# RWKV-6 time mixing and a ternary feed-forward on one core: a diagonal block copied earlier on GpSimd, and two elementwise steps moved from VectorE to GpSimd

## What is computed

```python
xx = x_prev - x                                  # difference of neighbouring tokens
mix = tanh((x + xx * time_maa_x) @ maa_w1)       # then, by five small matmuls, mw, mk, mv, mr, mg
xw, xk, xv, xr, xg = (x + xx * (time_maa_i + m_i) for each i)
r, k, v, g = xr @ Wr.T, xk @ Wk.T, xv @ Wv.T, silu(xg @ Wg.T)
decay = exp(-exp(time_decay + tanh(xw @ td_w1) @ td_w2))
# per token and head: y = r (S + u k v'),  S = decay * S + k v'
y = group_norm(y) * ln_g + ln_b
x = layernorm(x + (y * g) @ Wo.T)
h = layernorm(gelu(x @ ternary(W_fc).T)) @ ternary(W_proj).T
out = layernorm(x + h)
```

## Time and profile before

| | |
|---|---|
| median of 3 runs | 3076.63 us (3074.3 to 3081.04) |
| the profiled execution: own time | 3077.73 us |
| the profiled execution: span | 3075.9 us |
| PE busy | 2895.1 us (94%) |
| DVE busy | 2488.6 us (81%) |
| ACT busy | 1928.0 us (63%) |
| POOL busy | 931.3 us (30%) |
| granted TensorE clock, mean over the span | 0.991 |

### The profile page before, as it was taken

One profiled execution on the slowest core, in us unless ns is written; L12 is line 12 of the kernel. 1 busy time (PEld: TensorE's weight loads), 2 busy tenths in 40 slices (PEclk: granted clock), 3 DMA queues, 4 the chain that ended last, 5 costly groups with the idle time before them and its releaser, 6 DMA issues.

```text
span 3075.9 us, 101635 instructions
## 1 busy us (share of the span) xinstructions
PE 2895.1 (94%) x40249; PEld 2120.9 (69%) x40249; DVE 2488.6 (81%) x5435; ACT 1928.0 (63%) x4079; POOL 931.3 (30%) x790
## 2 busy tenths in 40 slices
PE   1889999999999999999999999999999999999997
PEld 0666677777677777677777676777677777767775
DVE  8467887788887788888788898788798788888777
ACT  0456676666676666676666576666567666667664
POOL 1223232333322333332233322233323233332232
PEclk9899999999999999999999999999999999999999
DMA  5000000000000000000000000000000000000000
GB/s 215 8 15 23 13 19 23 22 16 22 13 23 19 23 16 23 16 20 19 23 16 22 16 19 19 23 15 22 23 13 19 23 22 16 23 13 23 19 23 15
DMA packets 22822, 73.40 MB, mean 24 GB/s; under 512 B 3104, under 2 KB 3360, under 8 KB 20768
## 3 DMA queue, kind: packets, MB, share of 16 engines
q1 hardware_dynamic: 22432, 67.10, 6.4%
HBM read 50.31 MB, written 16.78 MB: 22 GB/s over the span
## 4 chain that ended last, share of the span: by engine, by line
PE 63%; DVE 23%; issue 9%; ACT 3%; DVEq 1%; DMA 1%; SPq 0%; ACTq 0%; POOLq 0%; POOL 0%
PE psP L404 18%; PE psF L641 11%; PE psP L442 7%; PE psP L616 6%; PE psF L660 4%; DVE HLO L1351 4%; DVE ARENA L1226 2%; PE psY L522 2%; PE psY L538 2%; DVE SUMS L1343 2%; DVE ARENA L1100 2%; DVE ARENA L1088 2%; DVE ARENA L1166 2%; DVE ARENA L1290 1%; PE psP L424 1%
## 5 line engine op out<-in xcount | busy, mean ns | idle before, releaser
L404 PE MATMUL psP<-ARENA,WALL 128*128 128x256 f32 x3072 | 694.2, 381 | 2.7 <-ACT ARENA L733 2.7
L690 ACT ACTIVATE ARENA<-ARENA 32x512 f32<-32x512 f32 (+3 forms) x930 | 524.2, 564 | 188.1 <-DVE ARENA L1166 92.5
L404 PEld LDWEIGHTS psP<-ARENA,WALL 128*128 128x128 f32 x3072 | 574.9, 190 | 79.3 <-issue 1.8
L1351 DVE SCALAR_TENSOR_TENSOR HLO<-GG,FWB,HHI 128x128 f16<-128x128 f32 x1024 | 347.5, 400 | 283.4 <-ACT HHI L861 278.4
L641 PE MATMUL psF<-XHI,WFC 128*128 128x128 f16 x4096 | 488.2, 220 | 2.2 <-DVE ST L1367 1.9
L641 PE MATMUL psF<-XLO,WFC 128*128 128x128 f16 x4096 | 486.6, 220 | 0.0
L902 POOL TENSOR_TENSOR MT<-ARENA 32x256 fp32r<-32x256 f32 x330 | 319.3, 968 | 445.3 <-ACT ARENA L690 416.7
L916 POOL TENSOR_TENSOR ARENA<-ARENA,XT 128x1024 f32<-128x1024 f32 x128 | 278.6, 2177 | 506.3 <-DVE ARENA L1100 506.3
L641 PEld LDWEIGHTS psF<-XHI,WFC 128*128 128x128 f16 x4096 | 397.9, 98 | 41.0 <-issue 32.9
L641 PEld LDWEIGHTS psF<-XLO,WFC 128*128 128x128 f16 x4096 | 402.0, 98 | 17.6 <-issue 10.3
L660 PE MATMUL psF<-WPJ,HHI 128*128 128x512 f16 x1024 | 390.6, 381 | 13.5 <-ACT GG L852 13.5
(11 more groups left out here) (165 smaller groups left out, 5160.4 us busy)
## 6 DMA issues: line engine op xcount, KB each, us to landing
XT<-x_ch SPq DMA_DIRECT2D x33, 520.0 KB, 3.4
ARENA<-x_tok SPq DMA_DIRECT2D x32, 512.0 KB, 4.7
out<-OUT SPq DMA_DIRECT2D x64, 256.0 KB, 2.1
WALL<-w_all SPq DMA_DIRECT2D x5, 1024.0 KB, 15.5
ARENA<-wfc SPq DMA_DIRECT2D x4, 1024.0 KB, 8.2
ARENA<-wpj SPq DMA_DIRECT2D x3, 1024.0 KB, 14.8
GG<-wpj SPq DMA_DIRECT2D x1, 1024.0 KB, 18.9
OUT<-w2a SPq DMA_DIRECT2D x8, 64.0 KB, 14.0
```

Source lines behind the costliest of these rows:

```text
L404: mm = pe.matmul(psP[:, P.bank(f"{name}{g}"), COLS * c:COLS * (c + 1)], WALL[:, w, k, 128 * (2 * g + c):128 * (2 * g + c + 1)], cc(XF[slot ...
L690: return act.activation(o, i, ACT.Copy)
L1351: e = dve.scalar_tensor_tensor(out=HLO[:, k, :], in0=GG[:, u % 2, 0, 128 * m:128 * (m + 1)], scalar=FWB[:, 0, k:k + 1], in1=HHI[:, k, :], ...
```

## The change

GpSimd gets `differences` for the next tile, behind the two bias additions and ahead of the diagonal block. Its copy of the diagonal block now stands ahead of the power on `FV`. Behind the power on the output's variance it gets the gate's scaling by ln_b, as one instruction over 1024 columns. VectorE loses both steps (except the differences of tile 0), and its `normed` and `up(1, 0)` change places. The semaphore for the scaled gate now counts one per tile.

```diff
@@ GpSimd
+            def differences(it):
+                pool.wait_ge(xt_in, 16 * (it + 1))
+                pool.tensor_tensor(XX[:, :, :], xprev, xcur, ALU.subtract).then_inc(xx_ready, 1)
...
                 if ffn:
                     ffn.bias()
-                    ffn.finish()
+                differences(it + 1)
 
 
                 pool.wait_ge(k1_odd, it + 1)
+                pool.wait_ge(xx_ready, it + 2)
                 if ffn:
                     ffn.settled()
                 pool.wait_ge(y_full, 2 * it + 1)
...
                 pool.wait_ge(ab_rest, it + 1)
+                if ffn:
+                    ffn.finish()
                 pool.wait_ge(tot_ready, NPL * it + 6)
...
                 if ffn:
                     ffn.normed()
+                pool.wait_ge(y_weighed, it + 1)
+                pool.tensor_tensor(G.rearrange("p (c t) -> p c t", c=KC), G.rearrange("p (c t) -> p c t", c=KC),
+                                   PAR[:, :, LN_B:LN_B + 1].broadcast_to([128, KC, COLS]), ALU.mult).then_inc(y_affine, 1)
 
                 pool.wait_ge(s_decayed, it + 1)
+                pool.wait_ge(y_affine, it + 1)
...
-                    pool.wait_ge(root_taken, 2 * PAIRS * j + 1)
+                    pool.wait_ge(root_taken, 2 * PAIRS * j)
@@ VectorE
                 if ffn:
                     ffn.stats()
-                dve.wait_ge(m_dve, M.read(it, "mg1"))
-                differences(it + 1)
                 if ffn:
                     ffn.finish()
                 outputs(1)
                 if ffn:
+                    ffn.up(1, 0)
                     ffn.normed()
-                if ffn:
-                    ffn.up(1, 0)
...
                 mixed_by_x(it + 1)
                 if ffn:
                     ffn.up(1, 1)
-                dve.wait_ge(y_weighed, it + 1)
-                for k in range(KC):
-                    dve.tensor_scalar(cc(G, k), cc(G, k), PAR[:, k, LN_B:LN_B + 1], None, ALU.mult).then_inc(y_affine, 1)
...
-                    dve.wait_ge(y_affine, KC * it + 4)
+                    dve.wait_ge(y_affine, it + 1)
```

## The result

The changed kernel takes 3107.91 us (median of 4 runs, 3105.44 to 3112.35), the kernel before 3075.68 us with one more run. The ratio is 1.0102, with a 95% interval of 1.009 to 1.0114: 1.0% slower, inside the range and on the side that was forecast. The profiled execution spans 3103.6 us.

The account below looks back on a forecast made before the run. TensorE sets the pace, with VectorE close behind through the levels. A front loss of 1.8 less a tail gain of 0.5 us, times 31 tiles, adds 40 us: 3117 us, 1.3% slower, range 3045 to 3140.

Parts of the forecast that it names:

- The wait ahead of L538 is the diagonal block, 1.46 us a tile.: TensorE's idleness before pair 1's L538: released by GpSimd's late diagonal block; removing it yields at most 45 us.
- The front costs 1.8 us a tile.: Next tile's start: GpSimd's differences delay VectorE's L1192, making L1156 1.79 us late and stalling TensorE.
- the hold of 2.05 us: Front: L1192 waits about 2.05 us for GpSimd's differences, sized by L1314 held inside L916; bounds 0 and 2.17.
- The slack of 0.26 us: Front: VectorE's only idle time before L1156, subtracted from the 2.05 us wait.
- Exclusion by reading, at both places: Front and tail: VectorE instructions with two SBUF inputs and SBUF-reading GpSimd instructions exclude each other; no exclusion at either, 12%.
- The tail gains 0.5 of the 1.46: Tile's tail: about 0.5 us a tile of TensorE's removed wait arrives; ends 0 and 1.4.
- L1088 waits for the gate: Tail: GpSimd's 1.95 us gate scaling holds VectorE's L1088 until 1536.5 instead of 1537.03.
- the signs that it is wrong: L1192 at 3.45 us with the differences beside it, or tail L1088 starting right behind the state's addition L1247.
- L1277 off VectorE is worth nothing.: Tail: removing these four VectorE instructions gives nothing, as they ran while VectorE waited for ScalarE's L852 and L861.
- the order of `normed` and L1351: Tail on VectorE: reversing these costs nothing, as L1351 waits only until 1530.85, 0.4 us of idle time.
- What would show it: Signs: L538's wait gone, differences 2.2 to 2.9 us, L1192's eight some 5.5, L464 waits 1 to 1.5, L1088 longer.
- the 1.3 forecast: Whole tile: front loss 1.8 minus tail gain 0.5 us, times 31 tiles, +40 us.

Follow-up runs that it names:

- e1: The kernel before with only GpSimd's diagonal block (ffn.finish) moved ahead of the power on the variance; ratio 0.9931, 3055.35 us.
- e6: The changed kernel with GpSimd's differences moved behind the power on the variance instead of ahead of the diagonal block; ratio 0.9958, 3061.13 us.
- e9: The changed kernel with GpSimd's differences done twice at the front, one behind the other; ratio 1.0263, 3158.72 us.
- e3: The changed kernel with differences back on VectorE, plus the same subtraction on GpSimd at the front, its result later overwritten; ratio 1.0103, 3106.56 us.
- e4: The changed kernel with differences back on VectorE, plus GpSimd memsets and two tiny subtractions at the front, results later overwritten; ratio 0.9945, 3060.06 us.
- e10: e8 with the gate's scaling on GpSimd and the changed kernel's order of the tail on VectorE; ratio 0.9945, 3057.74 us.
- e12: The changed kernel with the load of the tokens issued behind pair 1's product, nothing else; ratio 1.0093, 3102.85 us.
- e8: e7 with the load of the tokens issued behind pair 1's product; ratio 0.9855, 3030.76 us.
- e7: e1 with the differences on GpSimd behind the power; gate's scaling and tail order stay as before on VectorE; ratio 0.9911, 3048.36 us.
- e11: e7 with the load of the tokens at its early place but cut to 8 of 512 columns; ratio 0.9856, 3032.47 us.
- e5: e1 with SyncE's load of the tokens issued behind pair 1's product; ratio 0.9927, 3052.1 us.

## Why the prediction was right

Point by point, by its own steps:

- **The wait ahead of L538 is the diagonal block, 1.46 us a tile.** Right: 1.43 us between the two copies, and e1 shows it by itself.
- **The front costs 1.8 us a tile.** Right in place and mechanism, too large by 0.4: 1.38 us. The step that was mis-sized is the hold of 2.05 us, which came from L916's 2.17 us. The differences take 1.89 us alone (e6), and they held L1192 for 1.60. The rows give the rest: counted back by 1.89 us from its recorded end, GpSimd's instruction started 0.15 us ahead of the held one, and it let go 0.14 us ahead of that end, as L916 let go of L1314 by 0.12. The slack of 0.26 us was as read, and e9 shows that there is next to none behind it.
- **Exclusion by reading, at both places.** Shown for the front by e3 against e4. In the tail e10's rows show the hold on L1100 and none on L1259, which has one input in PSUM; no run had GpSimd only writing there.
- **The tail gains 0.5 of the 1.46.** It gained 0.30 on average, and the step "L1088 waits for the gate" holds in only 7 of 31 tiles. The gate's own times were as forecast: `y_weighed` came at 1545.33, 9.86 us behind the first copy (9.8 by the prediction's times), and the scaling took 1.90 us (1.95 said). What the prediction had put at nothing is TensorE's pause: the state's products came not at 10.06 us but at 10.97. In the other 24 tiles L1088 started right behind the state's addition and took 1.67 us, which the prediction lists among the signs that it is wrong. Its start at 11.71 us on average, where the prediction's 1536.5 - 1524.84 makes 11.66, is a coincidence. With the pauses all but gone (e12) the gate alone is the bound, L1340 comes at 14.29 us and the tail gains 0.53, the forecast figure; the pauses took the other 0.23. Two bounds stood within a few tenths of each other, and I had named one. With both away (e8) the tail gains 1.35 us (14.82 - 13.47).
- **L1277 off VectorE is worth nothing.** Right, to 0.07 us a tile by e10 against e8; with the hold that it brings it costs 27 us there. No run varied the order of `normed` and L1351 alone.
- **What would show it**: the eight of L1192 rose to 5.05 us (some 5.5 said), and GpSimd's differences have 2.99 us recorded as a median (2.2 to 2.9 said). At L464 TensorE's stall was at most 0.7 us (10.7 us in 31 waits among its weight loads), less than the 1 to 1.5 us forecast. Most of it came at L481, whose waits for L1188 grew by 33 us, 1.07 us a tile.

The sum: 1.38 - 0.30 = 1.08 us a tile for the 1.3 forecast, 3108 us for 3117. The forecast loss was 0.4 us too large and the forecast gain 0.2 us, so half of the first error was made good by the second; that the number came out so near is in part luck.

## What to carry to other kernels

Before moving an elementwise step from VectorE to GpSimd, lay its interval over VectorE's timeline and look at the operands beside it: where VectorE's instructions have two SBUF inputs, a GpSimd instruction that reads SBUF can cost VectorE most of its length (1.60 of 1.89 us here), and the step is better left where it was or put beside instructions that have an input in PSUM, or beside a wait. The same instruction of 1.9 us cost 1.4 us a tile at one place and nothing at another, some 32 us later in the tile. And when a wait is removed from the path, look at what the wait had hidden: here TensorE's pauses behind a load.

## What the runs showed of the hardware that I had not expected

Behind a load of 512 KB TensorE paused for up to 1.2 us in the middle of a group of matmuls, with no semaphore there, in a dense stretch of short instructions: 20.7 us in 25 pauses in the changed kernel, 10.1 us in 13 in e7, one pause in e8's L567 and none in e11. Moving the load alone moved the pause (e5), and cutting it to 8 KB took it away (e11).

I took it for TensorE's instruction supply held up behind the load. The load itself is not in flight any more: in the changed kernel its last packet had ended before each of the 25 pauses began. The duration of the instruction blocks' DMA records says nothing either (a median of 948 ns for the 36 that start within 5.5 us behind a load's issue, 1065 for the 343 others, in the changed kernel). Their start does. The blocks are 16 KB each; these are the starts of the one that falls near L641, in us behind the first copy of the product, in the 31 tiles:

```
kernel                early (2.0 to 3.0)   late (3.4 to 4.6)   pauses in L641
before                      12                  19                   0
changed                      5                  26                  25
e7_no_gate_on_pool          17                  14                  13
e11_small_xtok              31                   0                   0
```

In the changed kernel and in e7 each pause is in a tile with a late block and ends 2.2 to 2.5 us behind that block's start. In the kernel before, the block was as late in 19 tiles, and the stall ahead of L538 covered it. With the load at its later place it is the next block that counts. In e5 it starts late, at 7.8 to 8.4 us, in 22 tiles, of which 19 have the pause in L567, and at 6.1 to 6.3 in the 9 others, which have none. In e8 it is late in one tile alone, the one that pauses, and in 29 of the 30 others it has started by 6.1 us, about when the load's first packet does (6.0 to 6.2). So the same place of the load helps in e8 and not in e5 because the block gets in first there; pair 1's product, by the table, comes 0.2 us earlier in e8 than in e5, and this may be what decides it. That the load delays a block, and that TensorE waits for it, is by these rows the likely way. It is not proven: the records do not say which engine's instructions a block holds, and no run delayed a block without a load.
